# Projections held back behind the stack loads, and the maxima's rows formed on GpSimd from the fifth block on

## The reference, cut to what matters

```python
h = _layernorm(x) * (1 + ca) + sa
qkv = einsum('bsd,ed->bse', h, w_qkv) + b_qkv
scores = q @ k.T / sqrt(16) + causal        # 16 heads, 2048 x 2048
out = softmax(scores) @ v
x = x + ga * (out @ w_out.T + b_out)
h = _layernorm(x) * (1 + cb) + sb
# top-1 gate over 8 experts, capacity 320, then gelu(h @ wi) @ wo, scattered back
x = x + gb * expert_out
```

## Time and profile before

| | |
|---|---|
| timed runs | 782.27 us median of 3 (780.64 to 782.81) |
| profiled execution | 778.72 us, its span 777.0 us |
| mean granted TensorE clock | 0.927 of full |
| busy over the span | PE 676.4 us (87%), DVE 561.8 (72%), ACT 455.8 (59%), POOL 134.1 (17%) |

### The profile page before, as it was taken

The page is one execution under the profiler, slowest core; times in us unless marked ns, Lnnn a source line. Parts: engine busy times, 40 slices in busy tenths (PEclk is TensorE's granted clock), DMA queues, the critical chain, the costliest instruction groups (busy, mean ns, idle before and its releaser), DMA issues.

```text
span 777.0 us, 12195 instructions
## 1 busy us (share of the span) xinstructions
PE 676.4 (87%) x4290; PEld 370.4 (48%) x4290; DVE 561.8 (72%) x1467; ACT 455.8 (59%) x962; POOL 134.1 (17%) x194
## 2 busy tenths in 40 slices
PE   4686889489899999999999999988986279999994
PEld 3555444232333344333333333334533269999994
DVE  7763778468798987989998989974435447777762
ACT  1432546256577776777777777765761346666651
POOL 6000322130001122103221101100005300121122
PEclk9988889689899999999999999999987569999997
DMA  7435236531005123106800032000004283455200
GB/s 244 105 91 136 48 75 147 127 71 23 1 1 133 31 55 82 29 1 155 280 1 1 1 122 96 2 0 28 29 27 152 106 232 116 158 193 202 81 23 18
DMA packets 42111, 66.53 MB, mean 86 GB/s; under 512 B 3822, under 2 KB 31985, under 8 KB 41466
## 3 DMA queue, kind: packets, MB, share of 16 engines
q1 hardware_dynamic: 39746, 59.44, 27.3%
q0 software_dynamic: 2304, 6.31, 2.2%
HBM read 39.36 MB, written 26.78 MB: 85 GB/s over the span
## 4 chain that ended last, share of the span: by engine, by line
PE 69%; DVE 9%; issue 8%; ACT 7%; DMA 4%; POOL 1%; SPq 1%; DVEq 0%; POOLq 0%; ACTq 0%
PE bank L1280 15%; PE bank L1330 13%; PE bank L1358 13%; PE bank L1464 9%; PE bank L1447 8%; PE bank L1225 3%; ACT probs L842 3%; DMA qk_rows<-part 2%; PE bank L1383 2%; PE bank L1430 1%; DVE chunk_max L1089 1%; PE bank L1254 1%; PE bank L1407 1%; ACT stacks L831 1%; ACT qk_sb L792 1%
## 5 line engine op out<-in xcount | busy, mean ns | idle before, releaser
L842 ACT ACTIVATE probs<-bank 128x512 f32<-128x512 f32 (+3 forms) x640 | 295.2, 540 | 105.4 <-PE bank L1358 103.6
L1089 DVE TENSOR_REDUCE chunk_max<-bank 128x1 f32<-128x512 f32 x384 | 251.5, 685 | 30.4 <-PE bank L1330 28.7
L1358 PE MATMUL bank<-stacks 104*128 104x512 bf16 (+3 forms) x640 | 188.3, 358 | 19.6 <-DVE stacks L1115 12.3
L1330 PE MATMUL bank<-stacks 96*128 96x512 bf16 (+3 forms) x640 | 195.6, 359 | 7.1 <-DVE chunk_max L1089 4.0
L1280 PE MATMUL bank<-probs,v_sb 128*32 128x512 f32 (+3 forms) x1280 | 154.8, 557 | 0.4 <-POOL probs L738 0.4
L1095 DVE CUSTOM_DVE_ANT_0 masked<-bank,causal 128x128 bf16<-128x128 f32 (+3 forms) x256 | 120.7, 484 | 21.6 <-PE bank L1330 20.6
L1330 PEld LDWEIGHTS bank<-stacks 96*128 96x128 bf16 x640 | 55.6, 98 | 154.2 <-DVE chunk_max L1089 74.6
L738 POOL TENSOR_SCALAR_AFFINE_SELECT probs<-probs 128x512 f32<-128x512 f32 x64 | 40.8, 638 | 383.9 <-ACT probs L842 383.9
L1358 PEld LDWEIGHTS bank<-stacks 104*128 104x128 bf16 x640 | 63.1, 101 | 83.4 <-ACT probs L842 18.4
L1464 PE MATMUL bank<-w_split,acts 128*128 128x256 f32 x576 | 79.3, 283 | 0.0
L1464 PEld LDWEIGHTS bank<-w_split,acts 128*128 128x128 f32 x576 | 73.9, 189 | 1.5 <-issue 0.8
(11 more groups left out here) (140 smaller groups left out, 538.2 us busy)
## 6 DMA issues: line engine op xcount, KB each, us to landing
stacks<-qk_rows SPq DMA_DIRECT2D x6, 1536.0 KB, 12.2
w_raw<-w_in SPq DMA_DIRECT2D x8, 1024.0 KB, 5.0
w_raw<-w_down SPq DMA_DIRECT2D x8, 1024.0 KB, 8.1
qk_rows<-part SPq DMA_DIRECT2D x32, 192.0 KB, 2.8
slot_rows<-empty SPq DMA_DIRECT2D x1, 5140.0 KB, 28.9
slots_sb<-slot_rows SPq DMA_DIRECT2D x8, 514.0 KB, 4.2
qk_rows<-part SPq DMA_DIRECT2D x32, 128.0 KB, 2.4
stacks<-qk_rows SPq DMA_DIRECT2D x8, 384.0 KB, 4.3
```

Of the source, the lines that this page charges most:

```text
L842: act.activation(probs[:, s % 3, h, 0:width], of_ring(*ev)[:, 0:width], ACT.Exp)\
L1089: dve.tensor_reduce(to, src[:, 0:QB], AX.X, ALU.max).then_inc(max_read, 1)
L1330: pe.matmul(bank[MAX_BANKS[u % 3]][:, 0:width], stack(g, 0)[0:KR, h, q0:q0 + P], stack(g, 1)[0:KR, h, c * QB:c * QB + width], start=True, ...
L1358: pe.matmul(of_ring(*ev)[:, 0:QB - lo], stack(g, 1)[0:KR + MR, h, kt * P:(kt + 1) * P], stack(g, 0)[0:KR + MR, h, b * QB + lo:(b + 1) * QB ...
```

## The change

Three things are changed.

1. The planner holds back a group's projections until 15000 (`STACK_TIME - SPLIT_TIME`) after `parts_at` of the group before, that is 20000 after the end of that group's last projection.
2. From block n = 4 on (`PARTS_BY_POOL`), GpSimd instead of VectorE casts and subtracts the two parts, and copies the maxima's rows to the other heads. `neg_max` has two buffers now, and a new semaphore passes it from VectorE to GpSimd. VectorE waits before its reduction until the parts of two blocks earlier are formed. GpSimd's row copy waits for its own earlier masks, bias additions and rests, then for ScalarE's signal, and GpSimd then waits for the copy itself before it goes on.
3. The planner's estimates change to match. VectorE's cost of "max_parts" goes from 400 to 640 for the first four blocks and 220 afterwards, the rows count as formed 800 later from block 4 on, and as placed at 2700 instead of 1700. The cost of VectorE's row copy goes from 450 (not before now + 550) to 690 (not before now + 850) for the first four blocks, and to nothing afterwards.

```diff
+PARTS_BY_POOL = NB
...
             plan.append(("max_parts", n))
-            vector[-1] += 400
-            waiting_rows.append([n, vector[-1] + 100])
+            vector[-1] += 640 if n < PARTS_BY_POOL else 220
+            waiting_rows.append([n, vector[-1] + 100 + (0 if n < PARTS_BY_POOL else 800)])
...
-            placed_at[n] = now + 1700
-            vector[-1] = max(vector[-1], now + 550) + 450
+            placed_at[n] = now + (1700 if n < PARTS_BY_POOL else 2700)
+            if n < PARTS_BY_POOL:
+                vector[-1] = max(vector[-1], now + 850) + 690
...
-        if projections and not split and block >= PROJECT_FROM[projections[0][0]] and now >= projected + SPLIT_TIME:
+        stacks_on_way = projections and now < parts_at.get(projections[0][0] - 1, 0.0) + STACK_TIME - SPLIT_TIME
+        if projections and not split and not stacks_on_way and block >= PROJECT_FROM[projections[0][0]] \
+                and now >= projected + SPLIT_TIME:
...
+                if ev[0] == "max_parts" and ev[1] >= PARTS_BY_POOL:
+                    n = ev[1]
+                    neg = neg_max[:, n % 2, :]
+                    pool.wait_ge(neg_max_known, n + 1)
+                    pool.wait_ge(ring_filled, turn_of["max_rows", n - 2] + 1)
+                    link(pool.tensor_copy(max_part[:, n % 2, :, 0], neg))
+                    pool.tensor_tensor(max_part[:, n % 2, :, 1], neg, max_part[:, n % 2, :, 0], ALU.subtract)\
+                        .then_inc(max_parts, 1)
+                if ev[0] == "max_rows" and ev[1] >= PARTS_BY_POOL:
...
+                    pool.wait_ge(diag_done, masked_tiles)
+                    if biased:
+                        pool.wait_ge(x_biased, biased)
+                    pool.wait_ge(rest_ready_p, n_rests)
+                    if n_parts:
+                        pool.wait_ge(qk_split_p, n_parts)
+                    pool.wait_ge(max_row0, n + 1)
+                    pool.tensor_copy(rows[:, 1:HG, :], rows[:, 0:1, :].broadcast_to([MR, HG - 1, QB]))\
+                        .then_inc(max_rows, 1)
+                    pool.wait_ge(max_rows, n + 1)
...
                     if n >= 2:
-                        dve.wait_ge(ring_filled, turn_of["max_rows", n - 2] + 1)
-                    link(dve.tensor_copy(max_part[:, n % 2, :, 0], neg_max[:, :]))
-                    dve.tensor_tensor(max_part[:, n % 2, :, 1], neg_max[:, :], max_part[:, n % 2, :, 0], ALU.subtract)\
-                        .then_inc(max_parts, 1)
-                if ev[0] == "max_rows":
+                        dve.wait_ge(max_parts, n - 1)
+                    neg = neg_max[:, n % 2, :]
+                    dve.tensor_reduce(neg, chunk_max[:, n % 2, :, 0:b + 1], AX.X, ALU.max, negate=True)\
+                       .then_inc(neg_max_known, 1)
+                    if n < PARTS_BY_POOL:
...
+                if ev[0] == "max_rows" and ev[1] < PARTS_BY_POOL:
```

More of the change, by code:

```diff
@@ L415, in layer @@
         chunk_max = sb1("chunk_max", [P, 2, TB * HG, NB], F32)
-        neg_max = sb1("neg_max", [P, TB * HG], F32)
+        neg_max = sb1("neg_max", [P, 2, TB * HG], F32)
         max_part = sb1("max_part", [P, 2, TB * HG, 2], BF16)
@@ L477, in layer @@
         max_parts = sem("max_parts")
+        neg_max_known = sem("neg_max_known")
         max_row0 = sem("max_row0")
@@ L722, in _ @@
             pool.memset(empty[:, ROW - 1:ROW].bitcast(I32), S).then_inc(empty_ready, 1)
-            biased = 0
+            biased = masked_tiles = n_rests = n_parts = 0
             for ev in plan:
@@ L727, in _ @@
                     leave_part0(pool, ev[1] * NB + ev[2], rest_ready_p)
+                    n_rests += 1
                 if ev[0] == "split":
                     leave_part1(pool, ev[1] * NB + ev[2], qk_split_p)
+                    n_parts += 1
+                if ev[0] == "max_parts" and ev[1] >= PARTS_BY_POOL:
[7 more added lines that the diff above has]
+                if ev[0] == "max_rows" and ev[1] >= PARTS_BY_POOL:
+                    n = ev[1]
+                    g, b = divmod(n, NB)
+                    rows = stack(g, 0)[KR:KR + MR, :, b * QB:(b + 1) * QB]
+                    pool.wait_ge(diag_done, masked_tiles)
[8 more added lines that the diff above has]
+                    pool.wait_ge(max_rows, n + 1)
                 if ev[0] == "scores" and ev[3] == HG - 1:
@@ L739, in _ @@
                                            pattern=[[0, HG], [1, P]], channel_multiplier=-1).then_inc(diag_done, 1)
+                        masked_tiles += 1
                     if j >= 0 and BIAS_FROM <= n and biased < NT:
@@ L1102, in _ @@
                     dve.wait_ge(max_read, units_before[n + 1])
-                    link(dve.tensor_reduce(neg_max[:, :], chunk_max[:, n % 2, :, 0:b + 1], AX.X, ALU.max, negate=True))
                     if n >= 2:
-                        dve.wait_ge(ring_filled, turn_of["max_rows", n - 2] + 1)
-                    link(dve.tensor_copy(max_part[:, n % 2, :, 0], neg_max[:, :]))
-                    dve.tensor_tensor(max_part[:, n % 2, :, 1], neg_max[:, :], max_part[:, n % 2, :, 0], ALU.subtract)\
-                        .then_inc(max_parts, 1)
-                if ev[0] == "max_rows":
+                        dve.wait_ge(max_parts, n - 1)
[3 more added lines that the diff above has]
+                    if n < PARTS_BY_POOL:
+                        dve.wait_ge(neg_max_known, n + 1)
+                        if n >= 2:
+                            dve.wait_ge(ring_filled, turn_of["max_rows", n - 2] + 1)
+                        link(dve.tensor_copy(max_part[:, n % 2, :, 0], neg))
+                        dve.tensor_tensor(max_part[:, n % 2, :, 1], neg, max_part[:, n % 2, :, 0], ALU.subtract)\
+                            .then_inc(max_parts, 1)
+                if ev[0] == "max_rows" and ev[1] < PARTS_BY_POOL:
                     n = ev[1]
```

## The result

The changed kernel took 754.91 us (median of 4 runs, 751.42 to 759.41), the kernel before 782.54 us beside it. The ratio is 0.9651, with a 95% interval of 0.9593 to 0.9708. The forecast was 769.5 us in a range of 760 to 777: the sign was right and the gain, 27.6 us, more than twice the 12.8 that the sum gave. The profiled execution has a span of 752.1 us, against 777.0.

What follows compares the result with a forecast made beforehand. TensorE was taken to bound the steady part, VectorE close behind, with store-wait stalls around block 2. Holding projections back gave -12.8 us, GpSimd's work zero: 782.3 - 12.8 = 769.5 us, range 760 to 777.

Steps and rivals of the forecast that it cites:

- The two stalls: TensorE idle at block 2's first scores and at the block 1 to 2 change, behind L798's store waits: 9.6 and 2.7 us off.
- The clock: TensorE's half clock after each stall, 146.8 to about 151.5 and 158.5 to about 165 us, goes: 3.5 us off, bounds 0 and 5.5.
- that rival: The condition misses: stores still queue behind loads and the wait only moves; 0 to 4 us gained, 780 us, chance 0.05.
- The moved projections, +3.0: Two group 2 projections move behind the start of block 2's scoring and delay late maxima: 3.0 us cost, bounds 0 and 4.9.
- Part 1: Holding the projections back, in blocks 1 and 2: -9.6 - 2.7 - 3.5 + 3.0 = -12.8 us.
- block 3's maxima take it back: Rival: before block 3 all 4.9 us of moved work is lost and the low clock stays; -7.4, 775 us, chance 0.15.
- GpSimd's costs and saving: GpSimd forming parts and rows: costs 2.0 us, its copy taken at 1570 ns; VectorE's relief saves 2.0 us, bounds 0 and 20.9.
- the hidden bound: Rival: VectorE bounds the steady part, 49.73 of 55 us busy; about half of 20.9 us comes back, 759.5 us, chance 0.15.
- the masks were not held up: Rival judged: GpSimd's copy at 3.47 us overruns the 1.46 us slack before the weighing in 12 blocks; 793 us, chance 0.07.
- The wait of 2 us at block 15's first scores: TensorE already waits 1.17 us there for the rows; GpSimd's slower copy adds 0.9, making 2 us.
- the last line of part 2, "zero": GpSimd's work on parts and rows: costs 2.0, saving 2.0, net zero, bounds +8 and -10 us.
- The sign of error named in the forecast: The prediction is wrong if, among other signs, the span from 205 to 520 us shrinks or grows by over 3 us.

Runs made afterwards that it cites:

- c_only: The kernel before with only the planner's new condition on the projections; parts, rows and estimates as before. 766.27 us, ratio 0.9806.
- v_only: The kernel before, in its old order, with GpSimd forming parts and rows from block 4 on. 783.09 us, ratio 1.0029.
- cv: The kernel before with the projections' condition and GpSimd's work, old estimates for the order. 763.85 us, ratio 0.9786.
- e_only: The kernel before with the planner's new estimates alone; VectorE forms all parts and rows, projections not held back. 786.72 us, ratio 1.0067.
- hold_c: c_only plus one planner edit: tail output projection 3 held until block 14's heads are turned. 757.28 us, ratio 0.9706.
- late: The changed kernel with the new estimates for blocks 12 to 15 only, the old ones before. 753.42 us, ratio 0.9675.
- after: The changed kernel itself, all three changes, against the kernel before. 754.91 us, ratio 0.9651.
- after_again: The changed kernel run and profiled once more, on tail_late's chip, nothing altered. 755.67 us, ratio 0.9673.
- tail_late: The changed kernel with no tail work beside block 14; all twelve tiles' turning and output go beside block 15. 751.46 us, ratio 0.964.
- tail_late_b: The same kernel as tail_late, run and profiled a second time on another chip. 751.40 us, ratio 0.9628.

## Why the prediction was wrong

- **The two stalls: right. The clock: right in the sum, not in its places.** The stalls and the clock together had 15.8 us (9.6, 2.7 and 3.5). In c_only the step of block 1 fell from 46.5 to 36.5 and that of block 2 from 51.1 to 44.9, together 16.2 us. The condition does what it says, and that rival is out. But the steps don't size the terms one by one, since low stretches came and went that the forecast didn't have. In c_only TensorE works at 0.50 from 134.8 to 145.0 us, where it waits for its banks between block 2's last maxima; before, such a stretch began at 137.5 and was mostly hidden under the stall. And a third one of before, at the end of block 2, is gone (c_only has 1.00 there). From the start of the last matmul for block 3's maxima to the end of block 2, before took 9.5 us and c_only 8.0. Before, there:

```profile
197.00:199.00 2.00, 1.22 (x5) 0.59 (x6) 1.91 (x10) 0.58 (x2) 0.00 (x0) 0.50 0.00 0
199.00:201.00 2.00, 2.00 (x9) 0.51 (x11) 1.06 (x7) 1.50 (x4) 0.00 (x0) 0.50 0.00 0
```

- **The moved projections, +3.0: mis-sized.** Part 1 measured -16.2 us in blocks 1 and 2, and -16.8 with block 3, whose step went from 42.7 to 42.1 in c_only; the forecast was -12.8. Taken as the rest behind the 15.8 the term is about zero. With the third stretch's 1.5 us counted it would be about 1, an estimate from the steps above; no run sizes it alone. The rival by which block 3's maxima take it back fails with it.
- **GpSimd's costs and saving: right in themselves.** The copy took 1461 ns, and v_only (783.1) and cv (763.9) show zero, within 0.3%. VectorE was not the hidden bound, and the masks were not held up: TensorE waited 1.4 us for them between 259 and 482 us. The wait of 2 us at block 15's first scores didn't come: in the new order its rows were copied at 500.27 and its first scores began at 518.45. In the old order it was 1.2 us in v_only and 1.5 in cv, against 1.17 before. What was priced too low there is the parts' way through GpSimd's list: 0.3 to 0.8 us was taken, and in block 6 TensorE waited 2.0 and 2.1 us for them, in the changed kernel not at all.
- **The step that failed is the last line of part 2, "zero".** It priced the operations, and the planner's new numbers only as 1000 more allowed for the rows. They are inputs of an order. Maxima that end earlier, and tail tiles placed earlier, were never worked out, though planner and numbers stand in the diff. The runs showed -13.4 us in block 15 against +7 in blocks 4 to 14, so -6.3 where zero stood; e_only has the 13.4 by the order alone, and hold_c shows 8.6 of them to be the stall and the half clock behind it. The sign of error named in the forecast did show: from the end of block 2 to that of block 14, close to its 205 to 520 us, the time grew by 7.1 us, over the limit of 3.
- **Why nothing pointed at it.** I read the stretch from 520 us on only for block 15's first scores. The list of TensorE's waits there would have shown L1126, and the half clock behind it, as the dearest place left. The gain that was found was in the profile of before; the changed kernel reaches it by accident of its estimates, and hold_c most of it with two lines.
- **Sum.** Part 1 -16.7, blocks 3 to 14 +7.1, block 15 -13.4: -23.0. The stretch behind it gave 3.7 more and block 0 took 1.8, which makes the profiled -24.9. The median moved by 27.6: it lies 3.8 us above the profiled execution before and 1.1 after, where the forecast kept a distance of 3.6. No run ties the 3.7, the 1.8 or this 2.7 to a part of the change. The blocks' 23.0 alone would give 782.5 - 23.0 = 759.5 us, so the last 4.6 us of the miss may be chance.

## What to carry to other kernels

When a change touches the costs or due times of a planner, write out the order of before and after and look for what newly stands ahead of what; the operations' own price may be the small part. A short reading that was queued behind a long chain on another engine cost TensorE 3.7 us here and then a stretch at half clock, so look for such pairs in the list of waits of each stage, the last one too. And an order and the relief that makes it affordable are to be tested together and apart: alone, one was worth nothing here and the other was a loss.

## What the runs showed of the hardware

- GpSimd's copy of 8x1536 bf16 took 1461 or 1462 ns in each of 12, against a median of 689 on VectorE for the same shape. Its operations on 128x16 took 204 and 224 ns, where VectorE's took 179 and 180: for so small a tile the engine hardly matters.
- Some of VectorE's small operations on SBUF grew when one of GpSimd's ran beside them. Its cast of 128x16 has a median of 179 ns in e_only, and one took 1.10 us: it began 0.10 us into a subtraction of GpSimd's and ended 0.04 us behind it. Before, two of the same casts took 0.37 us beside a mask of GpSimd's and ended 0.03 to 0.04 us behind it (259.87 and 476.84), and L1115 took 0.93 and not 0.69 beside a subtraction. VectorE's reduction L1103 kept its 0.20 us beside the same two masks (259.63 and 476.61). That the overlap is the cause is read from the times and tested by no run. Timeline of e_only:

```profile
303.90 1.16 POOL L692 TENSOR_TENSOR part<-rest,part 128x512 bf16<-128x512 f32 x1 [2.46 <-ACT part L841]
304.00 1.10 DVE L1150 CAST max_part<-neg_max 128x16 bf16<-128x16 f32 x1
```

- One kernel's runs spread over some 8 us, with the granted clock moving along: in late they were 752.3, 752.4, 754.4 and 760.2 us, at granted clocks of 0.944, 0.942, 0.935 and 0.931. A median of 4 to 6 runs carries some of that. The steps between blocks decide here, and the medians support them: in after and after_again the two last steps agree to 0.01 us, though one step, block 6's, differs by 2.2 us between tail_late and tail_late_b.
